# Rotary half-swap of the third layer: from a permuting matmul on TensorE to a 32-partition shuffle on VectorE, with the step positions written anew

## The chip, the cores and the metric

One core of a Trainium2 chip runs the whole program. The metric is device time in microseconds (us) of one launch; lower is better. Engines are named as in the profile: PE (TensorE matmuls) and PEld (its weight loads), DVE (VectorE), ACT (ScalarE), POOL (GpSimd), SP (the engine that issues all DMAs here).

## The reference

Four conditioned layers follow each other on `x` of 8 sequences x 256 tokens x 512 features, all in float32. The third layer (`L == 2` in the kernel) is the one whose rotary step changes:

```
h = layernorm(x) * (1 + scale) + shift          # layer 2, B=2, T=512 in the reference's shapes
q = (h @ Wq.T)      -> 16 heads x 32
k = ((h @ Wkd.T) @ Wku.T) -> 4 kv heads x 32 ;  v = ((h @ Wkd.T) @ Wvu.T)
q = q * cos + rotate_half(q) * sin              # rotate_half: [-x[16:], x[:16]] in each head of 32
k = k * cos + rotate_half(k) * sin
y = softmax(q k^T / sqrt(32) + block/window mask) v ;  x = x + y @ Wo.T
```

Layer 0 is attention with heads of 64 and rotary (`rotate_half` over 32 and 32 features) and a gated SiLU MLP, layer 1 is cosine attention and a GELU MLP, layer 3 is eight small expert MLPs of 64 features, a normalisation and a projection.

## The kernel before

Features lie on the partitions and tokens on the free axis: `X` is 128 partitions x 4 feature blocks x 2048 tokens. The work is cut into 12 attention **items** (`ORDER`: layer, block of 512 tokens) of 16 **units** each; a unit is one softmax of one token half of one head group. Layer 2's items are the 8th and the 10th to 12th: `(2,0)`, `(2,1)`, `(2,2)`, `(2,3)`. Around the units lie the MLPs of layers 0 and 1 and, for layer 2's blocks, the expert layer (`first`, `second`), its normalisation (`z`) and the last projection (`last`).

There is one list of **steps**. `Plan.make` gives each step a position in units (the table `PLACE`, plus the unit number), sorts by it, and each engine then walks the same list and emits its own part of each step. So the position of a step sets where its instructions stand in each in-order queue, and which piece of an engine's work stands in front of which. The names of steps: `scores`, `softmax`, `normalise`, `turn` (transposes of the probabilities on PE, copied to `PT`), `values` make up a unit; `ro1` projects q or k into a PSUM bank (`B`) which ACT copies to a buffer in SBUF (`FB`, seven of them); `ro2` is the rotary step; `qs` and `ks` split q and k into a rounded high part and a remainder (`Q`, `KB`); `nsum` to `nfin` are the pieces of a normalisation (`nsub` writes `Y`, `nfin` writes `HA`, `HM` or `ZH`/`ZL`). Within one unit the DVE part of `ro2` stands behind the four masked score maxima of a `softmax` (`CUSTOM_DVE_ANT_0`, printed as `ISA` in the order rows) and ahead of the next `normalise`, whose reciprocal POOL needs to scale the probabilities (`SS`) that PE then transposes.

The rotary step of layer 2 before the change, in the order of its queues:

```
PE   waits a_raw:        matmul(bank, rotm, f)        # rotm: a 128x128 permutation m <-> m ^ 16, plain f32
DVE  waits p_rot:        g = bank * sin
POOL waits p_rot:        f = f * cos                  # beside DVE
DVE  waits d_sin, g_cos: f = f + g
```

It runs 20 times: four q tiles and one k tile for each of four items, each on 128x512. In layer 0 the first two k and five q tiles (7) use the same form with a permutation of 32, and 13 others get their swap by DMA (`swap`, `s_swap`), so that there both products read two SBUF operands. `rotm` is loaded twice, at the start and, in step `tables`, again with layer 2's permutation.

Of the kernel before, what the change touches and what calls it, by code (L numbers as in the profile page):

```python
# [11 lines left out]
ALU = mybir.AluOpType  # L12
# [18 lines left out]
PLACE = {  # L31
# [6 lines left out]
    "trig": [3.589, 20.401, 35.517],  # L38
    "out": [17.616, 33.486, 49.609, 65.605, 81.749, 97.151, 113.474, 129.833, 145.534, 161.755, 177.973, 191.6,
        194.705],  # L40
    "first": [137.43, 169.635, 179.31, 193.854, 198.087],
    "z norm": [141.577, 174.923, 183.064, 198.2, 201.446],
    "z final": [144.398, 176.596, 185.493, 204.08, 205.384],
    "last": [145.545, 178.406, 187.993, 205.459, 209.491],
    "q0 first": [-0.458, 0.616],
    "k0 first": [-0.054, 2.293, 1.626, 3.239],
    "q0": [-0.46, 1.879, 2.452],
    "k0": [0.356, 0.84, 1.722, 2.736, 4.534],
    "v0": [1.914],
    "q1": [-1.273, 0.351, 1.427],  # L50
    "k1": [0.902, 1.089, 2.211, 2.301, 3.616],
    "v1": [3.958, 4.1],
    "q2": [0.073, 1.078],
    "k2": [-0.167, 0.282, 4.809, 2.078, 2.91],
    "v2": [1.691],
    "out 2": [-0.233, -0.229, 0.066, 0.655],
    "experts": [0.513, 0.533, 1.635, 1.133, 0.603],
    "experts of one": [0.1, 0.5, 0.9, 0.875, 0.856],
# [4 lines left out]
    "last step": [0.67, 0.474],  # L63
    "a stats": [0.101, 0.101, 1.31, 1.42, 1.42, 1.791, 1.598, 2.652],
    "m stats": [-0.005, -0.005, 1.086, 0.92, 0.904, 1.25, 1.163, 1.935],
    "a parts": [1.109, 0.01, 0.128, 0.03],
    "a parts 0": [0, -0.073, 0.02, 0.449],
    "m parts": [0, 0.01, 1.323, 0.145],
    "m parts 0": [0, 0.01, 0.02, 0.03],
    "down": [0.802],  # L70
    "start": [-12.43, 6, -2.831, -0.049],
    "ada": [7.843, 21.989, 25.511, 29.324, 31.58, 34.532, 37.145, 40.064, 43.72, 46.196, 49.144],
}
# [32 lines left out]
PIECE = _piece_numbers()  # L106
LATENT = ("latent", 2, 0)


# [68 lines left out]
class Engine:  # L178
# [44 lines left out]
    def reciprocal(self, *a, **k):  # L223
        return self.real.reciprocal(*a, **k) if self.real is not None else self  # L224

    def dma_start(self, *a, **k):
# [3 lines left out]
def halves(ap):  # L230
    return ap.rearrange("p (b s) -> p b s", b=2)
# [82 lines left out]
class Plan:  # L314
# [63 lines left out]
    def projected(self, what, L, n, t):  # L378
        k = (what, L, n, t)
        if what == "k" and L == 2:  # L380
            self.banked("kd", n)
            yield
        f = self.f.take()
        if L == 1:
            g = self.f.take()
            self.banked("un1", k, f, g)
            yield
            self.banked("un2", k, g)
            yield
            self.banked("un3", k, f, g)  # L390
            self.f.give(g)
        else:
            if what == "k" and L == 0:
                self.raw_values[n] = self.f.take()
                self.banked("kv", k, f, self.raw_values[n])
            else:
                self.banked("ro1", k, f)
            yield
            g = self.f.take()
            if swapped_by_dma(L, n, t):  # L400
                self.add("swap", k, f, g)
                yield
                self.add("ro2", k, f, g, None)
            else:
                self.banked("ro2", k, f, g)
            self.f.give(g)
        if what == "q":
            self.add("qs", k, f)
            self.f.give(f)
            yield  # L410
        else:
            yield
            self.add("ks", k, f, 0)
            yield
            self.add("ks", k, f, 1)
            self.f.give(f)
            yield
# [319 lines left out]
def program(nc, xT, pos, condT, biasd, cols, consts, tab2, wpack, adaw, out):  # L737
    ctx = ExitStack()
    with ctx:
# [3 lines left out]
        def tally(name, step=1):  # L743
            return Tally(ctx.enter_context(nc.semaphore(name)), step)
# [25 lines left out]
        rotm = sb("rotm", [128, 128])  # L770
# [14 lines left out]
        fr = Pool([FB[:, i, :] for i in range(FBUFS)])  # L785
# [3 lines left out]
        def col(name, i=0):  # L789
# [29 lines left out]
        d_nmul, d_nlo = tally("d_nmul"), tally("d_nlo")  # L819
        d_trig, d_sin, d_qk, d_qhi, d_khi = (tally(x) for x in ("d_trig", "d_sin", "d_qk", "d_qhi", "d_khi"))  # L820
        d_klo, d_qmax, d_ck = tally("d_klo"), tally("d_qmax"), tally("d_ck")
        d_max, d_neg, d_rec, d_pt, d_cx = (tally(x) for x in ("d_max", "d_neg", "d_rec", "d_pt", "d_cx"))
# [10 lines left out]
            a_y, d_ada, d_sm, d_gb, d_sum, d_sub, d_sq, d_var, d_nmul, d_nlo, d_trig,  # L833
            d_sin, d_qk, d_qhi, d_khi, d_klo, d_qmax, d_ck, d_max, d_neg, d_rec, d_pt, d_cx, d_xo, d_gate, d_glo,
            d_xd, d_tg, d_xl, g_const, g_whi, g_wlo, g_rstd, g_cos, g_qlo, g_qr, g_norm, g_xb]
# [113 lines left out]
        def tensor(e):  # L949
# [18 lines left out]
            for step in weights.steps:  # L968
# [65 lines left out]
                elif kind == "ro2":  # L1034
                    k, f, g, u = a
                    if u is not None:
                        e.wait_ge(*s_rot.of(k[1]))
                        e.wait_ge(*a_raw.of(*k))
                        e.wait_ge(*dp.over(u))
                        e.matmul(dp.buf(u)[:, :], rotm[:, :], fr.buf(f),  # L1040
                                 start=True, stop=True).then_inc(*p_rot.up(*k))
# [167 lines left out]
        def vector(e):  # L1209
            e.wait_ge(*s_cv.of())  # L1210
            e.wait_ge(*g_const.of(1))
            for step in weights.steps:
# [125 lines left out]
                elif kind == "ro2":  # L1338
# [5 lines left out]
                    e.wait_ge(*(a_sin.of(n) if L == 0 else s_tab.of()))  # L1344
                    if u is None:
                        e.wait_ge(*s_swap.of(*k))
# [354 lines left out]
        def gpsimd(e):  # L1701
            for step in weights.steps:
# [32 lines left out]
                elif kind == "ro2":  # L1735
# [4 lines left out]
                           TR[:, 0, 0:256].unsqueeze(1).broadcast_to([128, 2, 256]))  # L1740
                    e.wait_ge(*(p_rot if u is not None else s_swap).of(*k))
                    e.wait_ge(*(a_cos.of(n) if L == 0 else s_tab.of()))
# [26 lines left out]
        def sync(e):  # L1769
            for step in weights.steps:  # L1770
# [38 lines left out]
                elif kind == "tables":  # L1809
                    e.wait_ge(*d_qk.of("q", 0, 3, 3))  # L1810
                    e.dma_start(rotm[:, :], consts[2]).then_inc(*s_rot.up(2))
                    e.dma_start(TR[:, 0, :], tab2[0]).then_inc(*s_tab.up(0))
# [169 lines left out]
```

## Time and profile before

| what | value |
|---|---|
| runs of the kernel before | 2055.98, 2043.96, 2051.99 us; median 2051.99 |
| span of the profiled execution | 2053.7 us (the profile gives no other time for it) |
| PE busy, PEld busy | 1912.4 us (93%), 1512.5 us (74%) |
| DVE, ACT, POOL busy | 1110.8 (54%), 1027.7 (50%), 795.9 us (39%) |
| the chain that ended last, by engine | PE 76%, DVE 10%, POOL 4%, ACT 4%, issue 3%, DMA 1% |

The span is the time from the first to the last instruction of one execution. "Busy" is the share in which an engine had an instruction running. The chain is followed back from the last instruction, at each step to what released it; its shares say where a microsecond saved or added counts at once.

### The profile page before, as it was taken

How to read it: one execution, taken by the hardware profiler on the slowest of the kernel's cores; microseconds unless marked ns; L12 is line 12 of the kernel's file. 1: busy time of each engine (PE TensorE's matmuls, PEld its weight loads, DVE VectorE, ACT ScalarE, POOL GpSimd, SP SyncE). 2: the span in 40 equal slices, each digit the busy share in tenths (PEclk: the TensorE clock that was granted, in tenths of full speed). 3: DMA queues.
4: the chain of work that ended last, by engine and by line, in shares of the span. 5: the costliest groups of instructions: out<-in, count | busy, mean ns of one | idle time of the engine just before them, and what ended most of it. 6: DMA issues, size and time to landing. Idle time of an engine off the chain costs nothing.

```text
span 2053.7 us, 35242 instructions
## 1 busy us (share of the span) xinstructions
PE 1912.4 (93%) x12880; PEld 1512.5 (74%) x12880; DVE 1110.8 (54%) x3184; ACT 1027.7 (50%) x2474; POOL 795.9 (39%) x1094
## 2 busy tenths in 40 slices
PE   5889999999999999999899989989999989988987
PEld 3567777788888878887778777768876768855565
DVE  5655535644553365345664676574554675366363
ACT  3542423433343344443565465555567565468665
POOL 4556662111124243234667554326332432243230
PEclk9899999999999999999999999989999999989989
DMA  7336677555444534444345433433433335322311
GB/s 249 110 129 209 229 249 264 181 196 190 172 160 177 181 134 171 156 158 153 135 174 187 158 118 139 171 114 107 165 113 134 127 110 195 130 81 69 124 63 52
DMA packets 98795, 314.84 MB, mean 153 GB/s; under 512 B 11584, under 2 KB 13376, under 8 KB 97088
## 3 DMA queue, kind: packets, MB, share of 16 engines
q1 hardware_dynamic: 98624, 312.58, 43.7%
q8 instruction: 104, 1.70, 0.3%
q14 instruction: 67, 0.55, 0.1%
HBM read 242.55 MB, written 66.58 MB: 151 GB/s over the span
## 4 chain that ended last, share of the span: by engine, by line
PE 76%; DVE 10%; POOL 4%; ACT 4%; issue 3%; DMA 1%; SPq 0%; POOLq 0%; DVEq 0%; ACTq 0%
PE B L194 69%; PE B L197 7%; DVE FB L215 2%; POOL R L212 1%; DVE SS L218 1%; DVE T L212 1%; POOL SS L209 1%; ACT SS L200 1%; DVE FB L212 1%; POOL FB L212 1%; DMA ST<-in_wpack 1%; DVE PT L206 1%; ACT FB L200 1%; DVE HA L215 1%; POOL W L212 1%
## 5 line engine op out<-in xcount | busy, mean ns | idle before, releaser
L209 POOL TENSOR_SCALAR SS<-SS,NM 128x256 f32<-128x256 f32 (+1 forms) x640 | 290.2, 471 | 747.3 <-DVE NM L224 747.1
L194 PE MATMUL B<-HM,W 128*128 128x512 f32 x2304 | 540.1, 395 | 9.2 <-DVE HM L215 5.7
L194 PEld LDWEIGHTS B<-HM,W 128*128 128x128 f32 x2304 | 436.5, 190 | 105.6 <-issue 5.0
L194 PE MATMUL B<-G,W 128*128 128x512 f32 x1536 | 391.6, 405 | 8.1 <-POOL W L212 4.3
L194 PEld LDWEIGHTS B<-G,W 128*128 128x128 f32 x1536 | 286.1, 191 | 76.1 <-issue 10.7
L200 ACT ACTIVATE SS<-SS,NM 128x256 f32<-128x256 f32 (+1 forms) x512 | 240.5, 471 | 121.2 <-DVE NM L218 120.8
L194 PE MATMUL B<-HA,W 128*128 128x512 f32 x864 | 229.6, 418 | 6.1 <-DVE HA L212 4.4
L197 PE MATMUL B<-ident,SS 128*128 128x128 f32 x1152 | 180.6, 294 | 41.1 <-POOL SS L209 33.6
L194 PEld LDWEIGHTS B<-HA,W 128*128 128x128 f32 x864 | 170.6, 202 | 45.9 <-issue 5.4
L212 DVE TENSOR_TENSOR G<-FB,G 128x512 fp32r<-128x512 f32 x128 | 99.5, 780 | 165.3 <-ACT G L200 165.2
L197 PEld LDWEIGHTS B<-ident,SS 128*128 128x128 f32 x1152 | 129.9, 147 | 77.6 <-issue 41.1
L212 POOL TENSOR_TENSOR R<-R,few 128x16 f32<-128x16 f32 (+2 forms) x57 | 119.3, 2095 | 141.5 <-DVE R L209 141.4
L200 ACT ACTIVATE PT<-B 128x512 f32<-128x512 f32 x160 | 95.0, 593 | 149.6 <-PE B L197 147.4
L212 POOL TENSOR_TENSOR W<-ST,W 128x512 fp32r<-128x512 f32 x119 | 159.8, 1343 | 9.9
L200 ACT ACTIVATE G<-FB 128x512 fp32r<-128x512 f32 x128 | 80.9, 632 | 162.3 <-DVE FB L212 160.3
L209 POOL TENSOR_SCALAR W<-ST 128x512 fp32r<-128x512 f32 x119 | 80.3, 675 | 201.4 <-PE B L194 125.2
L212 DVE TENSOR_TENSOR FB<-FB,B 128x512 f32<-128x512 f32 x64 | 44.0, 687 | 191.5 <-PE B L194 175.8
L200 ACT ACTIVATE FB<-B 128x512 f32<-128x512 f32 (+2 forms) x148 | 85.6, 592 | 105.3 <-PE B L194 104.8
L194 PE MATMUL B<-CX,W 128*128 128x512 f32 (+1 forms) x624 | 136.3, 376 | 0.3 <-issue 0.3
L212 DVE TENSOR_TENSOR X<-X,B 128x512 f32<-128x512 f32 (+1 forms) x100 | 66.4, 665 | 128.8 <-PE B L194 128.7
L200 ACT ACT_TABLE_LOAD x99 | 127.0, 1283 | 4.8 <-PE B L194 2.4
L194 PEld LDWEIGHTS B<-CX,W 128*128 128x128 f32 x624 | 111.3, 190 | 22.8 <-issue 1.9
(109 smaller groups left out, 2654.0 us busy)
## 6 DMA issues: line engine op xcount, KB each, us to landing
W<-kept SPq DMA_DIRECT2D x357, 512.0 KB, 4.2
kept<-W SPq DMA_DIRECT2D x119, 512.0 KB, 4.6
ST<-in_wpack SPq DMA_DIRECT2D x139, 256.0 KB, 2.9
Y<-in_adaw SPq DMA_DIRECT2D x12, 1024.0 KB, 6.8
FB<-FB SPq DMA_DIRECT2D x52, 64.0 KB, 2.6
X<-in_xT SPq DMA_DIRECT2D x1, 3072.0 KB, 13.0
out_xT<-X SPq DMA_DIRECT2D x12, 256.0 KB, 2.1
FB<-in_pos SPq DMA_DIRECT2D x4, 256.0 KB, 6.0
```

Of the source, the lines that this page charges most:

```text
L194: return self.real.matmul(*a, **k) if self.real is not None else self
L197: return self.real.transpose(*a, **k) if self.real is not None else self
L200: return self.real.activation(*a, **k) if self.real is not None else self
L206: return self.real.tensor_copy(*a, **k) if self.real is not None else self
L209: return self.real.tensor_scalar(*a, **k) if self.real is not None else self
L212: return self.real.tensor_tensor(*a, **k) if self.real is not None else self
L215: return self.real.scalar_tensor_tensor(*a, **k) if self.real is not None else self
L218: return self.real.tensor_tensor_reduce(*a, **k) if self.real is not None else self
```

## The change

In layer 2 the PE matmul with `rotm` is gone. DVE swaps the halves itself with `stream_shuffle`, which permutes within each group of 32 partitions, from the buffer `f` into `g`, and then multiplies `g` by sin in place. POOL's product with cos now waits for the shuffle (it overwrites `f`, which the shuffle reads). The second load of `rotm` is gone. Layer 0 is as it was.

```diff
+SWAP_16 = [i ^ 16 for i in range(32)]
@@ Plan.projected
             if swapped_by_dma(L, n, t):
                 self.add("swap", k, f, g)
                 yield
                 self.add("ro2", k, f, g, None)
+            elif L == 2:
+                self.add("ro2", k, f, g, None)
             else:
                 self.banked("ro2", k, f, g)
@@ vector, step ro2
-                    if u is None:
+                    if L == 2:
+                        e.wait_ge(*a_raw.of(*k))
+                        e.wait_ge(*fr.over(gu))
+                        e.stream_shuffle(g, f, SWAP_16).then_inc(*d_swap.up(*k))
+                        e.wait_ge(*d_swap.of(*k))
+                        e.tensor_tensor(halves(g), halves(g), sin, ALU.mult).then_inc(*d_sin.up(*k))
+                    elif u is None:
@@ gpsimd, step ro2
-                    e.wait_ge(*(p_rot if u is not None else s_swap).of(*k))
+                    e.wait_ge(*(d_swap if L == 2 else p_rot if u is not None else s_swap).of(*k))
@@ sync, step tables
-                    e.dma_start(rotm[:, :], consts[2]).then_inc(*s_rot.up(2))
@@ PLACE (a few of the rows; nearly all changed by some hundredths to one unit)
-    "a norm": [3.377, 19.79, 36.916, ...
+    "a norm": [1.615, 20.526, 36.655, ...
-    "q0 first": [-0.458, 0.616],
+    "q0 first": [-0.361, 0.592],
-    "k1": [0.902, 1.089, 2.211, 2.301, 3.616],
+    "k1": [0.968, 1.082, 2.418, 2.301, 3.651],
-    "k2": [-0.167, 0.282, 4.809, 2.078, 2.91],
+    "k2": [-0.336, 1.352, 2.401, 1.944, 2.516],
-    "z stats": [-0.298, -0.298, 0.784, 0.657, 0.657, 1.406, 1.406, 2.27],
+    "z stats": [-0.319, -0.279, 0.835, 0.826, 0.567, 0.948, 1.536, 2.362],
-    "start": [-12.43, 6, -2.831, -0.049],
+    "start": [-12.532, 5.863, -1.544, 1.755],
```

The list of steps keeps its length; some 270 of the 2592 steps stand elsewhere, most of them by a few steps. Three places in DVE's queue are shown, all on one engine, since it is the one on which the new work lands.

**The start, first item.** DVE's queue from the first score maxima of unit 0 (`TENSOR_REDUCE NM<-B`) on. The first q tile is done; `FB<-B,TR` and what follows is the rotary step of the second q tile, `RECIPROCAL` is `normalise` of unit 0. Before:

```order
L221 TENSOR_REDUCE NM<-B 128x1 [waits p_sc]
L221 TENSOR_REDUCE NM<-B 128x1
L209 TENSOR_SCALAR NM<-NM 128x2 [waits d_max]
L212 TENSOR_TENSOR FB<-B,TR 128x512 [waits a_cos,p_rot]
L212 TENSOR_TENSOR FB<-FB 128x512 [waits g_cos,d_sin]
L206 CAST Q<-FB 128x512 [waits d_qk]
L224 RECIPROCAL NM<-NM 128x2 [waits a_exp]
```

and of the change:

```order
L222 TENSOR_REDUCE NM<-B 128x1 [waits p_sc]
L222 TENSOR_REDUCE NM<-B 128x1
L210 TENSOR_SCALAR NM<-NM 128x2 [waits d_max]
L225 RECIPROCAL NM<-NM 128x2 [waits a_exp]
L222 TENSOR_REDUCE NM<-B 128x1 x2
L210 TENSOR_SCALAR NM<-NM 128x2 [waits d_max]
L225 RECIPROCAL NM<-NM 128x2 [waits a_exp]
L222 TENSOR_REDUCE NM<-B 128x1 [waits p_sc]
L222 TENSOR_REDUCE NM<-B 128x1
L210 TENSOR_SCALAR NM<-NM 128x2 [waits d_max]
L213 TENSOR_TENSOR FB<-B,TR 128x512 [waits a_cos,p_rot]
```

The rotary step of the second q tile has moved from ahead of the first reciprocal to behind the second one.

**The k tile of the last item, (2,3).** DVE's queue at the last two of four score maxima of an even unit, then the rotary step of k and its split into `KB`. Before:

```order
L218 ISA SS,NM<-B,TR 128x128
L218 ISA NM 128x1
L212 TENSOR_TENSOR FB<-B,TR 128x512 [waits d_nlo,p_rot]
L212 TENSOR_TENSOR FB<-FB 128x512 [waits g_cos,d_sin]
L209 TENSOR_SCALAR KB<-FB 128x256 [waits d_qk]
L215 SCALAR_TENSOR_TENSOR KB<-FB,KB 128x256 [waits d_khi]
L209 TENSOR_SCALAR KB<-FB 128x256
L215 SCALAR_TENSOR_TENSOR KB<-FB,KB 128x256 [waits d_khi]
L224 RECIPROCAL NM<-NM 128x2 [waits a_exp] x2
```

and of the change, from the first q tile of the same item on:

```order
L228 STREAM_SHUFFLE FB<-FB 128x512 [waits a_raw]
L213 TENSOR_TENSOR FB<-FB,TR 128x512 [waits d_swap]
L213 TENSOR_TENSOR FB<-FB 128x512 [waits g_cos,d_sin]
L207 CAST Q<-FB 128x512 [waits d_qk]
L228 STREAM_SHUFFLE FB<-FB 128x512 [waits d_nlo,a_raw]
L213 TENSOR_TENSOR FB<-FB,TR 128x512 [waits d_swap]
L213 TENSOR_TENSOR FB<-FB 128x512 [waits g_cos,d_sin]
L225 RECIPROCAL NM<-NM 128x2 [waits a_exp] x2
L219 ISA SS,NM<-B,TR 128x128 [waits p_sc,g_norm]
L219 ISA NM 128x1
```

Each rotary step has one DVE instruction more, and k's stands one unit earlier, right behind q's; only its split into `KB` is left behind the score maxima.

**The second q tile of item (2,3).** DVE's queue from the rotary step on; `Y<-Y,B` are the four subtractions of the normalisation `z` of block 1. Before:

```order
L212 TENSOR_TENSOR FB<-B,TR 128x512 [waits d_nlo,p_rot]
L212 TENSOR_TENSOR FB<-FB 128x512 [waits g_cos,d_sin]
L206 CAST Q<-FB 128x512 [waits d_qk]
L212 TENSOR_TENSOR Y<-Y,B 128x512 [waits p_tot]
L212 TENSOR_TENSOR Y<-Y,B 128x512 x3
L224 RECIPROCAL NM<-NM 128x2 [waits a_exp] x2
```

and of the change:

```order
L228 STREAM_SHUFFLE FB<-FB 128x512 [waits d_nlo,a_raw]
L213 TENSOR_TENSOR FB<-FB,TR 128x512 [waits d_swap]
L213 TENSOR_TENSOR FB<-FB 128x512 [waits g_cos,d_sin]
L207 CAST Q<-FB 128x512 [waits d_qk]
L225 RECIPROCAL NM<-NM 128x2 [waits a_exp] x2
L219 ISA SS,NM<-B,TR 128x128 [waits p_sc,g_norm]
L219 ISA NM 128x1
```

The four subtractions have moved from ahead of the reciprocals to behind the next score maxima. At the same point of the next q tile but one, with block 2's subtractions, nothing has moved.

## Rows read from the trace of the kernel before

**Rows 1.** The page: span, and busy time by engine.

```profile
span 2053.7 us, 35242 instructions
PE 1912.4 (93%) x12880; PEld 1512.5 (74%) x12880; DVE 1110.8 (54%) x3184; ACT 1027.7 (50%) x2474; POOL 795.9 (39%) x1094
```

**Rows 2.** Windows: stretch, its length, busy us by engine, clock, DMA share, GB/s.

```profile
1240.00:1790.00 550.00, 527.35 (x3730) 415.71 (x3729) 315.89 (x1033) 318.11 (x786) 194.01 (x309) 0.97 0.39 138
1790.00:2054.00 264.00, 221.71 (x1669) 153.13 (x1667) 134.36 (x465) 172.43 (x443) 70.39 (x133) 0.90 0.23 77
```

**Rows 3.** Timeline of PE around two rotary matmuls: start, length, instruction.

```profile
1552.74 1.02 PE L194 MATMUL B<-FB,rotm 128*128 128x512 f32 x2
1553.69 1.13 PE L194 MATMUL B<-X,ST 64*128 64x512 f32 x4
...
1912.19 0.39 PE L194 MATMUL B<-ZH,W 128*128 128x512 f32 x1
1912.42 1.02 PE L194 MATMUL B<-FB,rotm 128*128 128x512 f32 x2
1912.87 0.80 PE L194 MATMUL B<-ZH,W 128*128 128x512 f32 x1
1913.51 0.40 PE L194 MATMUL B<-ZL,W 128*128 128x512 f32 x1
```

**Rows 4.** The chain that ended last, at rotary steps: start, length, engine.

```profile
1349.59 1.27 POOL FB L212
...
1801.60 0.61 DVE FB L212
...
1909.82 5.24 PE B L194 x21
...
1952.97 0.61 DVE FB L212
```

**Rows 5.** Timeline of DVE: two rotary steps of layer 2.

```profile
1852.28 0.69 DVE L212 TENSOR_TENSOR FB<-B,TR 128x512 f32<-128x512 f32 x1
1852.99 0.69 DVE L212 TENSOR_TENSOR FB<-FB 128x512 f32<-128x512 f32 x1
...
1913.47 0.69 DVE L212 TENSOR_TENSOR FB<-B,TR 128x512 f32<-128x512 f32 x1
1914.92 0.69 DVE L212 TENSOR_TENSOR FB<-FB 128x512 f32<-128x512 f32 x1 [0.76 <-POOL FB L212]
```

**Rows 6.** Timeline of DVE and POOL: two rotary steps of layer 0 after a DMA swap.

```profile
117.51 0.68 DVE L212 TENSOR_TENSOR FB<-FB,TR 128x512 f32<-128x512 f32 x1
117.55 1.80 POOL L212 TENSOR_TENSOR FB<-FB,TR 128x512 f32<-128x512 f32 x1
...
240.22 1.29 POOL L212 TENSOR_TENSOR FB<-FB,TR 128x512 f32<-128x512 f32 x1 [2.15 <-DMA FB<-FB]
240.24 1.82 DVE L212 TENSOR_TENSOR FB<-FB,TR 128x512 f32<-128x512 f32 x1 [0.63 <-DMA FB<-FB]
```

**Rows 7.** Groups by line and form: busy us, mean ns of one, idle before.

```profile
L206 DVE COPY PT<-B 128x512 f32<-128x512 f32 x128 | 87.7, 685 | 39.6 <-PE B L197 39.5
L206 DVE CAST Q<-FB 128x512 fp32r<-128x512 f32 x48 | 20.6, 428 | 1.6
```

**Rows 8.** Timeline of PE: the first transposes of probabilities.

```profile
46.16 1.11 PE L197 MATMUL B<-ident,SS 128*128 128x128 f32 x4 [3.78 <-POOL SS L209]
```

**Rows 9.** The chain at the second rotary step of item (2,3).

```profile
1877.90 2.47 DVE Y L212 x4
```

**Rows 10.** The chain ahead of the first up-projection of layer 1.

```profile
980.32 0.97 DVE KB L209
...
981.95 0.87 DVE FB L215 x2
```

**Rows 11.** Timeline of DVE: the k tile of item (2,3).

```profile
1861.81 0.29 DVE L218 CUSTOM_DVE_ANT_0 SS<-B,TR 128x128 f32<-128x128 f32 x1 [7.53 <-PE B L194]
...
1863.14 0.69 DVE L212 TENSOR_TENSOR FB<-B,TR 128x512 f32<-128x512 f32 x1 [0.39 <-PE B L194]
```

More of the change, by code:

```diff
@@ L31 @@
 PLACE = {
[6 rows of a table removed]
[L38 to L44, printed above, removed]
-    "q0 first": [-0.458, 0.616],
-    "k0 first": [-0.054, 2.293, 1.626, 3.239],
@@ L47 @@
[L47 to L50, printed above, removed]
-    "k1": [0.902, 1.089, 2.211, 2.301, 3.616],
-    "v1": [3.958, 4.1],
-    "q2": [0.073, 1.078],
-    "k2": [-0.167, 0.282, 4.809, 2.078, 2.91],
[L55 to L58, printed above, removed]
[4 rows of a table removed]
-    "last step": [0.67, 0.474],
-    "a stats": [0.101, 0.101, 1.31, 1.42, 1.42, 1.791, 1.598, 2.652],
@@ L65 @@
[L65 to L69, printed above, removed]
[6 rows of a table added]
+    "trig": [3.757, 20.79, 35.346],
+        "out": [17.562, 33.986, 49.665, 65.869, 81.465, 97.161, 114.6, 129.42, 145.624, 161.915, 178.22, 191.644,
+        194.786],
+    "first": [137.423, 169.635, 179.31, 193.787, 198.265],
+    "z norm": [140.957, 175.185, 183.101, 198.014, 201.221],
@@ new lines @@
+    "z final": [144.289, 176.77, 185.552, 203.718, 205.5],
+    "last": [145.658, 178.299, 187.993, 206.303, 209.503],
+    "q0 first": [-0.361, 0.592],
+    "k0 first": [-0.233, 2.603, 1.16, 3.296],
+    "q0": [-0.503, 1.822, 2.318],
+    "k0": [0.161, 0.313, 1.159, 2.7, 4.778],
+    "v0": [1.932],
+    "q1": [-1.242, 0.3, 1.457],
+    "k1": [0.968, 1.082, 2.418, 2.301, 3.651],
+    "v1": [3.967, 4.146],
+    "q2": [0.145, 1.054],
+    "k2": [-0.336, 1.352, 2.401, 1.944, 2.516],
+    "v2": [1.589],
@@ new lines @@
+    "out 2": [-0.25, -0.2, 0.3, 0.6],
+    "experts": [0.515, 0.535, 1.5, 1.135, 0.605],
+    "experts of one": [0.075, 0.228, 0.851, 0.829, 0.818],
[4 rows of a table added]
+    "last step": [0.67, 0.355],
+    "a stats": [0.082, 0.144, 1.119, 1.387, 1.337, 1.78, 1.579, 2.691],
+    "m stats": [-0.14, 0.078, 1.086, 0.825, 0.904, 1.25, 1.16, 1.992],
+    "a parts": [0.863, 2.514, 1.443, -0.016],
+    "a parts 0": [1.686, -0.064, -0.015, 0.53],
+    "m parts": [0.008, -0.048, 1.986, 0.187],
+    "m parts 0": [-0.021, 0.957, 0.919, 0.038],
@@ L70 @@
     "down": [0.802],
-    "start": [-12.43, 6, -2.831, -0.049],
-    "ada": [7.843, 21.989, 25.511, 29.324, 31.58, 34.532, 37.145, 40.064, 43.72, 46.196, 49.144],
+    "start": [-12.532, 5.863, -1.544, 1.755],
+    "ada": [8.231, 22.321, 26.715, 29.81, 31.968, 34.92, 37.498, 40.455, 44.123, 46.8, 49.75],
 }
@@ L224, in reciprocal, with stream_shuffle @@
         return self.real.reciprocal(*a, **k) if self.real is not None else self
+    def stream_shuffle(self, *a, **k):
+        return self.real.stream_shuffle(*a, **k) if self.real is not None else self
     def dma_start(self, *a, **k):
@@ L820, in program @@
         d_trig, d_sin, d_qk, d_qhi, d_khi = (tally(x) for x in ("d_trig", "d_sin", "d_qk", "d_qhi", "d_khi"))
+        d_swap = tally("d_swap")
         d_klo, d_qmax, d_ck = tally("d_klo"), tally("d_qmax"), tally("d_ck")
@@ L833, in program @@
             a_y, d_ada, d_sm, d_gb, d_sum, d_sub, d_sq, d_var, d_nmul, d_nlo, d_trig,
-            d_sin, d_qk, d_qhi, d_khi, d_klo, d_qmax, d_ck, d_max, d_neg, d_rec, d_pt, d_cx, d_xo, d_gate, d_glo,
+            d_swap, d_sin, d_qk, d_qhi, d_khi, d_klo, d_qmax, d_ck, d_max, d_neg, d_rec, d_pt, d_cx, d_xo, d_gate, d_glo,
             d_xd, d_tg, d_xl, g_const, g_whi, g_wlo, g_rstd, g_cos, g_qlo, g_qr, g_norm, g_xb]
@@ L1036, in tensor @@
                     if u is not None:
-                        e.wait_ge(*s_rot.of(k[1]))
+                        e.wait_ge(*s_rot.of(0))
                         e.wait_ge(*a_raw.of(*k))
@@ L1950 @@
         np.full((128, 1), math.pi / 2), np.tile(np.repeat([-1.0, 1.0], 32), 2)[:, None]], axis=1)
-    consts = np.zeros((3, 128, 128), f)
+    consts = np.zeros((2, 128, 128), f)
     consts[0] = np.eye(128)
     for m in range(128):
-        consts[1, m ^ 32, m] = consts[2, m ^ 16, m] = 1.0
+        consts[1, m ^ 32, m] = 1.0
     i = np.arange(256)
```

18 rows, old and new, of the table PLACE are left out of this document.

## The prediction

> **What bounds the kernel now.** I read the page first, then the windows by stage, then the chain of waits at each of the 20 places that the change touches, then the timeline there. The page says that PE has a matmul running in 93% of the 2053.7 us and no other engine in more than 54% [rows 1]. So a removed matmul is worth its time wherever PE has no wait close by, and DVE has room on average. The windows correct this for the end: from 1240 to 1790 us PE is busy 527 of 550, but after 1790 us, where no MLP work is left to fill in, PE is busy 222 of 264 us [rows 2], and the waits there are for one unit's softmax to go around DVE, ACT, POOL and PE. The profiled execution's only own time is its span of 2053.7 us; the median of the runs shown is 1.7 us less, so I make the sum against the span and take 1.7 off. The three runs spread over 12 us, so about 0.5% (10 us) is what a measurement of this kernel can tell from no change.
>
> **What the change takes from PE.** One swap is two matmul instructions on 128x512, 20 swaps in all. The busy time of 1.02 us overlaps with its neighbours, so I take the delay of the next work. Around 1912 us the instruction before the swap gave way after 0.23 us, the swap itself after 0.45, and the first product behind it after 0.64 in place of 0.23: 0.45 + 0.64 - 0.23 = 0.86 us. Where a plain f32 product follows, as at 1552.74, it starts 0.95 us after the swap [rows 3]. I looked up the chain at all 20 places: at 14 the swap lies inside a stretch of the chain on PE (the last of them is the stretch at 1909.82), at six (1347, 1596, 1799, 1819, 1873 and 1949 us) it doesn't [rows 4]. Of the 14, ten are of the first kind and four of the second: 10 x 0.86 + 4 x 0.95 = **-12.4 us**. For the other six I take nothing, since PE waits for DVE or POOL there anyway; all twenty at 0.95 would be -19, the far end. The second load of `rotm` held up nothing; nothing for that.
>
> **What it adds on DVE.** Before, DVE is held for one rotary step from the start of its product to the end of its sum. This comes in two sizes: 1852.28 to 1853.68 is 1.41 us where POOL had its product done before (14 of the 20), and 1913.47 to 1915.61 is 2.14 us where the sum waits 0.76 for POOL (6 of 20) [rows 5]. The change makes all 20 alike, because POOL's product can't start before DVE's shuffle is done. The trace has no shuffle. The nearest rows are the 128x512 copy from PSUM with 685 ns and the 128x512 cast within SBUF with 428 ns [rows 7]; I take 0.69, because nothing shows that a permutation runs at the cast's rate, and keep 0.43 as the low end.
>
> Behind the shuffle, both products read two SBUF operands and are released by the same semaphore. That is what layer 0 does after its DMA swaps, and its rows show that the two then don't run side by side: at 117.51 DVE starts first, and POOL's product, elsewhere 1.29 us, takes 1.80; at 240.22 POOL starts 0.02 earlier, and DVE's product, elsewhere 0.68, takes 1.82 [rows 6]. In the first case POOL ends at 119.35, and with 0.10 to the sum and its 0.69 the pair and the sum take 2.63 us; in the second DVE ends at 242.06, and they take 2.54. Before the change, DVE's product in layer 2 read PSUM and ran beside POOL's without loss. So a rotary step will hold DVE for 0.69 + 0.05 + 2.6 = **3.3 us**, which is 1.9 more in the 14 cases and 1.2 more in the six: 14 x 1.9 + 6 x 1.2 = 34 us of DVE time. Were the products side by side, it would be 0.69 + 0.05 + 1.29 + 0.10 + 0.69 = 2.8.
>
> The Trainium skill ("SBUF — State Buffer", the part on the two physically separate sides) has the rule behind this: VectorE and GpSimd share one pair of SBUF ports, an instruction of VectorE with two SBUF inputs takes it as an exclusive lock against a GpSimd instruction that reads SBUF, and the later one blocks until the earlier has ended. By that rule the sum below has 8.8 us for DVE; with 2.8 us per step, which one would take without it, it would have 6.3. The trace agrees with the rule in layer 0, with 1.80 and 1.82 us.
>
> **Where DVE's extra time counts.** The reciprocal for POOL and the split for the scores stand behind each step, so it counts where the chain runs through the rotary step. That is so at 1349, 1801, 1821, 1863, 1876 and 1952 us [rows 4]. The first was of the longer kind, +1.2; four of the rest were of the shorter, 4 x 1.9 = 7.6; together **+8.8 us**. The one at 1863 is k's, which is moved (below). At the other 14 I price it at nothing: the chain there is on PE's products, which run on while DVE is held. If that cover is gone everywhere, it is the full 34.
>
> **What the moved steps bring.** The shift of all places goes both ways, and I price only those that stand at a PE wait.
> - Start: PE waits 3.78 us for the first scaled probabilities [rows 8]. The reciprocal in front of them stood behind a rotary step of 2.1 us and a cast of 0.43 [rows 5, 7]; it no longer does: -2.6, between 0 and -2.6, because a projection of 12 matmuls has moved into the same wait.
> - Up-projection of layer 1 at 986 us: the chain runs through a split of k for 1.6 us, from 980.32 to 981.95 [rows 10]. By the new `k1` and `m final` it stands behind the first two parts of the normalisation: -1.6, or 0 if the second part is then late by as much.
> - The four subtractions at 1877.90, 2.5 us on the chain [rows 9], stand behind reciprocals and maxima now: -2.5.
> - k of the last item: its wait of 0.39 and its step of 2.1 us lay on the chain; one unit earlier it falls into an idle time of DVE of 7.5 us, of which it needs 3.3 [rows 5, 11]: -2.5.
>
> Sum of these: **-9.2**, from 0 to -9.2. SP's queue has the large load of `X` one place earlier and one load less; no wait of PE is on either.
>
> **The sum.** -12.4 + 8.8 - 9.2 = -12.8 us: 2053.7 - 12.8 = 2040.9 as a span, less 1.7 is **2039 us**, 0.6% faster.
>
> **The rivals.**
> 1. *The forecast*: PE's time is saved at some two thirds of the places, DVE gives part of it back at five, the moves repair the worst. 2039; its own range 2031 to 2045. Chance 0.45.
> 2. *The moved steps bring nothing.* Half of the list's shifts have no row that speaks for them, and a wait that goes from one place can come back one unit later. Without the 9.2: 2053.7 - 12.4 + 8.8 - 1.7 = 2048, within 0.5%. For it: two of my four prices are upper bounds. Chance 0.27.
> 3. *DVE's cost is hidden almost everywhere and the moves help more than I can price.* -19 + 0 - 9.2 gives 2024; halfway between this and the forecast 2031. For it: DVE has 46% idle, and a whole table of places was set to suit the new lengths. Chance 0.18.
> 4. *DVE becomes the bound of layer 2's units* (the other side). Place: each rotary step of (2,0) to (2,3), ahead of the reciprocal that POOL waits for and PE's transposes behind it. It decides once PE's queue behind those transposes is shorter than the 1.9 us added. PE's idle time after 1790 us is already 42 us in 264 [rows 2]. If 34 us count in full against 12.4 and the moves bring 0: 2053.7 + 21.6 - 1.7 = 2074; if two thirds of it do, +10, 2062. Against it: between 1240 and 1790 us PE is idle for 23 of 550 us only [rows 2], and at 11 of the 13 rotary steps there the chain is on PE. Chance 0.10.
>
> That the change doesn't do what it says I exclude: DVE's queue has 20 shuffles and PE's 20 rotary matmuls fewer. The range takes the first three rivals and half of the way to the fourth: 2026 to 2055. From the cases, faster by over 0.5% (below 2041.7) has 0.18 + two thirds of 0.45 + a little of rival 2 = 0.53, within 0.5% 0.37, slower 0.10.
>
> **What would show it.** Right: 14 `rotm` matmul instructions are left of 54; PE's busy time falls by about 20 us; a shuffle takes about 0.69 us; DVE's or POOL's product behind it takes 1.8 in place of 0.69 or 1.3; from shuffle to the end of the sum 3.3 us in all 20. PE's wait at 46 us is shorter by 2 to 3 us, and that at 986 by up to 1.6. Wrong: the shuffle is 1 us or more (each 0.3 us is 1.5 on the path, six in all); PE's idle time in 1240 to 1790 us grows from 23 us by more than 5, which is rival 4; or the stretch 120 to 1240 us, where nothing of the swap lies, is longer by more than 3 us, which would mean that the moved steps hurt.

## The result, and the profile after

The changed kernel takes 2061.64 us (median of 4 runs, 2059.84 to 2063.22) where the kernel before takes 2047.97 (median of 4, 2042.92 to 2055.98): ratio 1.0064, 95% interval [1.0037, 1.0091]. It is slower by 0.6%, some 13 us. The forecast was 2039 us with a range that ended at 2055. A span is about 2 us shorter than its launch (2059.8 against 2061.57 here), so the profiled execution of before, with a span of 2053.7 us, is the longest of its four launches, 8 us above their median. So the two spans differ by only 6 us; for sizes I use medians and ratios.

The page of the changed kernel: span, busy time, and the chain that ended last by engine.

```profile
span 2059.8 us, 35190 instructions
PE 1891.5 (92%) x12840; PEld 1499.2 (73%) x12840; DVE 1130.3 (55%) x3224; ACT 1027.1 (50%) x2474; POOL 802.5 (39%) x1094
...
PE 72%; DVE 11%; POOL 5%; ACT 4%; issue 4%; DMA 2%; SPq 0%; DVEq 0%; POOLq 0%; ACTq 0%
```

PE is busy 21 us less than in [rows 1] and yet the span is longer. The windows say where its idle time grew (columns as in [rows 2]).

```profile
1240.00:1790.00 550.00, 516.57 (x3664) 407.76 (x3664) 321.71 (x1047) 318.25 (x793) 200.60 (x307) 0.97 0.40 138
1790.00:2059.80 269.80, 215.00 (x1642) 148.71 (x1640) 139.96 (x478) 170.01 (x433) 71.91 (x130) 0.88 0.24 75
```

PE's idle time is 33.4 us in the first stretch (before 22.7) and 54.8 in the second (before 42.3). That is 23 us more, and more than the 21 us by which PE's busy time fell. The cast to `Q` behind the first rotary step of item (2,0) starts at 1243.50 (before 1246.05), so the changed kernel enters layer 2 with a lead of 2.6 us; the one behind the last step of (2,3) starts at 1960.49 (before 1954.33). All of the loss comes in between.

The new instructions, by source line (duration in ns: shortest, median, longest), and who waited for them:

```profile
L228 DVE LOAD_MASK_SELECT FB<-FB x20: 12/14/15, 1240.1 to 1957.1; - x20
L228 DVE STREAM_SHUFFLE FB<-FB x20: 721/732/752, 1240.1 to 1957.1; 128x512 f32<-128x512 f32 x20
...
  POOL FB L213: 55.2, 18
```

Timeline of DVE and POOL at the rotary step that [rows 5] shows first:

```profile
1852.40 0.01 DVE L228 LOAD_MASK_SELECT FB<-FB  x1
1852.40 0.74 DVE L228 STREAM_SHUFFLE FB<-FB 128x512 f32<-128x512 f32 x1
...
1853.17 0.69 DVE L213 TENSOR_TENSOR FB<-FB,TR 128x512 f32<-128x512 f32 x1
...
1853.22 1.77 POOL L213 TENSOR_TENSOR FB<-FB,TR 128x512 f32<-128x512 f32 x1 [12.14 <-DVE FB L228]
...
1855.10 0.69 DVE L213 TENSOR_TENSOR FB<-FB 128x512 f32<-128x512 f32 x1 [1.23 <-POOL FB L213]
```

From the start of the shuffle to the end of the sum DVE is held 3.39 us (1852.40 to 1855.79), before 1.41. Over the 20 steps it is 3.37 to 3.94, in sum 69.5 us (before 32.5): 37 us more. I call this sum the **held time** below.

What a longer hold does is seen at 1801 us of [rows 4]. The chain of the changed kernel, from the last score maximum ahead of the rotary step to the transposes behind it:

```profile
1798.13 0.28 DVE SS L219
1798.42 0.73 DVE FB L228
1799.15 0.07 issue
1799.22 1.78 POOL FB L213
...
1801.10 0.70 DVE FB L213
...
1801.83 0.44 DVE Q L207
...
1802.33 1.27 POOL Q L213
1803.60 3.12 POOL SS L210 x4
...
1806.77 1.55 PE B L198 x6
```

Product and sum took 1.33 us of the chain before (0.61, 0.02 and 0.70); the same stretch is now 3.38 us, from 1798.42 to 1801.80, and it also pushes POOL's scaling of the probabilities (`SS`). PE's timeline shows the wait at two of these places:

```profile
1805.01 0.69 PE L198 MATMUL B<-ident,SS 128*128 128x128 f32 x2 [3.61 <-POOL SS L210]
...
1826.79 0.69 PE L198 MATMUL B<-ident,SS 128*128 128x128 f32 x2 [4.52 <-POOL SS L210]
```

Before, PE waited 0.85 and 1.96 us there. In the list of waits of the whole execution the same pairs have grown: for PE's transposes from 33.6 us in 21 waits, for the rotary sum from 24.2, for ACT's exponentials behind the masked maxima from 120.8:

```profile
ACT SS L201 <- DVE NM L219: 148.8, 96, 6.2
...
DVE FB L213 <- POOL FB L213: 44.2, 30, 8.8
...
PE B L198 <- POOL SS L210: 39.7, 24, 6.5
```

### The profile page after: what moved, and what is told of

Same layout as the page of the kernel before. It is cut to its first block, busy times and chain, and to the rows that moved or that the text cites. A ratio compares the mean times of both kernels' runs of the same rounds, so it can differ in the third digit from the quotient of the medians.

```text
span 2059.8 us, 35190 instructions
## 1 busy us (share of the span) xinstructions
PE 1891.5 (92%) x12840; PEld 1499.2 (73%) x12840; DVE 1130.3 (55%) x3224; ACT 1027.1 (50%) x2474; POOL 802.5 (39%) x1094
## 4 chain that ended last, share of the span: by engine, by line
PE 72%; DVE 11%; POOL 5%; ACT 4%; issue 4%; DMA 2%; SPq 0%; DVEq 0%; POOLq 0%; ACTq 0%
PE B L195 66%; PE B L198 6%; DVE SS L219 2%; POOL FB L213 2%; DVE FB L216 2%; DMA ST<-in_wpack 1%; POOL SS L210 1%; POOL R L213 1%; DVE T L213 1%; ACT SS L201 1%; DVE PT L207 1%; ACT FB L201 1%; DVE FB L213 1%; POOL W L213 1%; DVE X L216 1%
## 5 line engine op out<-in xcount | busy, mean ns | idle before, releaser
L195 PE MATMUL B<-HA,W 128*128 128x512 f32 x864 | 223.9, 409 | 9.8 <-DVE HA L213 4.5
L195 PEld LDWEIGHTS B<-HA,W 128*128 128x128 f32 x864 | 165.9, 197 | 48.7 <-issue 4.2
```

What stands on the lines that cost most here:

```text
L195: return self.real.matmul(*a, **k) if self.real is not None else self
```

## The experiments

My theory after the result: the time for which DVE is held decides, at all 20 steps and not only at the five that I priced; removed PE time and moved steps bring less than I took them for. The rival: the new places of the steps cost what the shuffle gains. Ratios are to the kernel before, with 95% intervals; 0.001 is 2.05 us, and "held" in a result is the held time of the 20 steps in that run's trace.

### The two halves of the change apart

`e1_places` is the kernel before with the new table `PLACE`; `e2_shuffle` is the changed kernel with the old table.

> The kernel before with the new table of places and nothing else: the matmul swap stays. Theory P (the new places lose time by themselves): ratio to before at 1.005 or more, most of the measured 1.0064. Theory D (the places are about neutral or a small gain, and the rotary step on VectorE costs more than TensorE saves): 0.995 to 1.001, and the PE waits that the prediction priced are shorter (46 us by 2 to 3 us, 986 us by 1 to 2, the one after 1877 us by 2).

> The changed kernel with the table of places of before: the shuffle alone. Theory D: slower than before, 1.003 to 1.010, with PE's busy time down by 20 us and PE's idle time up by more than that, most of it after 1240 us; a rotary step holds DVE for 3.3 us. Theory P: 0.992 to 0.998, since 12 us of TensorE time are gone from the path and DVE has room.

Measured: places alone **1.0001** [0.9988, 1.0014], shuffle alone **1.0086** [1.0064, 1.0108]. The rival is out: the places cost nothing that can be told (the interval is 2.7 us either way), and the whole loss is the shuffle's, with 69.2 us held. With the new places it is 1.0064; the intervals overlap, so whether they repair some of it isn't told.

### What the removed matmul is worth, and what an added one costs

`e3_narrow` keeps the rotary matmul of layer 2, on 64 of its 512 columns (the swap of the other columns is left out); `e12_double` does it twice.

```diff
@@ tensor, step ro2 (e3_narrow)
-                        e.matmul(dp.buf(u)[:, :], rotm[:, :], fr.buf(f),
+                        z = slice(0, 64) if k[1] == 2 else slice(0, 512)
+                        e.matmul(dp.buf(u)[:, z], rotm[:, :], fr.buf(f)[:, z],
@@ tensor, step ro2 (e12_double)
+                        if k[1] == 2:
+                            e.matmul(dp.buf(u)[:, :], rotm[:, :], fr.buf(f), start=True, stop=True)
```

> The kernel before, with layer 2's 20 rotary matmuls on 64 of their 512 columns (the other columns of the bank are then not the swapped halves, so this part of the computation is left out); DVE and POOL do what they did. It takes about seven eighths of the 18 us off TensorE and adds nothing anywhere. If the prediction's 12.4 us on the path is right: 0.994 to 0.996 (8 to 12 us faster). If TensorE's time is mostly not on the path (the removed matmuls are given back as waits at once): 0.998 to 1.001.

> The kernel before with each of layer 2's 20 rotary matmuls done twice on PE (the same result), so 18 us more on TensorE and nothing else. If 14 of the 20 are on the path, as the prediction read from the chain: +12 us, 1.005 to 1.007. If the narrow matmul told right that only a quarter to a third of such time counts: +4 to +6 us, 1.002 to 1.003.

Measured: 7/8 of the matmul away **0.9981** [0.9966, 0.9996], -3.9 us for 15 to 17 us of PE (7/8 of 20 x 0.86 to 0.95); done twice **1.0071** [1.0052, 1.0091], +14.6 us for 17 to 19. By this run my -12.4 was about three times too large. Per microsecond of PE the two directions differ (0.25 and 0.8), by more than their intervals allow.

### The hold of DVE, shortened with the shuffle kept

POOL's product with cos goes to a third buffer. It needs no longer wait for the shuffle, only for `a_raw`, and has ended when DVE comes. `e4_third` has the old places, `e5_third_places` the new, and `e8_before_third` is the kernel before with the third buffer.

```diff
@@ e5_third_places against the changed kernel; some lines left out
-                self.add("ro2", k, f, g, None)
+                h = self.f.take()
+                self.add("ro2", k, f, g, h)
+                self.f.give(h)
@@ vector, step ro2
-                    e.tensor_tensor(f, f, g, ALU.add).then_inc(*d_qk.up(*k))
+                    e.tensor_tensor(f, fr.buf(u) if L == 2 else f, g, ALU.add).then_inc(*d_qk.up(*k))
@@ gpsimd, step ro2
-                    e.wait_ge(*(d_swap if L == 2 else p_rot if u is not None else s_swap).of(*k))
+                    e.wait_ge(*(a_raw if L == 2 else p_rot if u is not None else s_swap).of(*k))
-                    e.tensor_tensor(halves(f), halves(f), cos, ALU.mult).then_inc(*g_cos.up(*k))
+                    if L == 2:
+                        e.wait_ge(*fr.over(u))
+                    e.tensor_tensor(halves(fr.buf(u)) if L == 2 else halves(f), halves(f), cos, ALU.mult).then_inc(*g_cos.up(*k))
```

> As the shuffle alone with before's places, but POOL writes its product with cos into a third buffer of FB, so it waits for the copy of the projection and not for the shuffle, and mostly runs before DVE gets there. A rotary step then holds DVE for about 0.73 + 0.69 + 0.69 = 2.2 us in place of 3.3. Theory D with the port lock and the late product of POOL as the larger part: at least 8 us faster than the shuffle alone and no slower than before (0.994 to 1.000). If the shuffle's own time or the places are to blame: within 3 us of the shuffle alone.

> The changed kernel, places and all, with POOL's product in a third buffer. If the places are neutral here as they were with the matmul swap: like the third buffer with before's places, 0.997 to 1.001, so 10 to 17 us faster than the changed kernel. If the new places suit a long rotary step and no other: 1.002 to 1.006.

> The kernel before, matmul swap and places kept, with POOL's product in a third buffer and waiting for the copy of the projection only. The six rotary steps in which DVE waited 0.76 us for POOL lose that wait: at most 4.5 us less holding. Theory D1: 0.998 to 1.000. It also says how much of the third buffer's gain is POOL's and how much is that the shuffle needs it.

Timeline of DVE in `e4_third`, at the same step as above:

```profile
1845.60 0.73 DVE L228 STREAM_SHUFFLE FB<-FB 128x512 f32<-128x512 f32 x1
...
1846.36 0.69 DVE L213 TENSOR_TENSOR FB<-FB,TR 128x512 f32<-128x512 f32 x1
...
1847.09 0.69 DVE L213 TENSOR_TENSOR FB<-FB 128x512 f32<-128x512 f32 x1
```

The hold is 2.18 us here (1845.60 to 1847.78), 47.0 in all, and the loss is gone: **0.9997** [0.9979, 1.0015]. With the new places it is 0.9993 [0.9980, 1.0005] (held 48.9), and the third buffer in the kernel before gives 0.9998 [0.9987, 1.0010]. So 22 us less of held time went with 18 us less of time: 0.8 each. None of the three can be told from the kernel before. Two things change at once here: DVE is held less, and POOL's product is done early and no longer stands late in POOL's own queue, ahead of its scaling of the probabilities. These runs don't separate the two.

### The hold lengthened with the matmul kept

In `e6_copy_late` DVE copies the matmul's bank to `g` ahead of its product, and POOL waits for the copy, as it does for the shuffle; in `e7_copy` POOL waits for the matmul as before.

```diff
@@ vector (e6_copy_late and e7_copy)
+                        if L == 2:
+                            e.tensor_copy(g, dp.buf(u)[:, :]).then_inc(*d_swap.up(*k))
+                            e.wait_ge(*d_swap.of(*k))
@@ gpsimd (e6_copy_late only)
-                    e.wait_ge(*(p_rot if u is not None else s_swap).of(*k))
+                    e.wait_ge(*(d_swap if L == 2 else p_rot if u is not None else s_swap).of(*k))
```

> The kernel before with the matmul swap kept, and in layer 2 one DVE copy of the bank to SBUF ahead of the product with sin, for which POOL's product waits as it does for the shuffle. The product with sin still reads the bank in PSUM, so two long products with two SBUF operands never meet: the late product of POOL without the port lock. A rotary step should hold DVE for about 2.8 us. Theory D1 (DVE's holding time is what costs, whatever it is made of; 17.6 us at +34 to +37 us of holding, plus what TensorE gave back): with +24 us of holding about 13 us slower than before, 1.005 to 1.008. Theory D2 (the lock has an effect beyond its time): under 1.004.

> As the run with the copy, but POOL's product waits for the matmul as before. Only 20 x 0.7 us of DVE time are added; DVE is held for 2.1 us in the cases that were short, and for 2.1 to 2.8 in the others. Theory D1: about 6 to 8 us slower than before, 1.002 to 1.005. If DVE's 46% of idle time hides it, as the prediction priced the places off the chain: under 1.002.

Timeline of DVE and POOL in `e6_copy_late`:

```profile
1848.94 0.69 DVE L206 COPY FB<-B 128x512 f32<-128x512 f32 x1
1849.66 0.69 DVE L212 TENSOR_TENSOR FB<-B,TR 128x512 f32<-128x512 f32 x1
1849.71 1.27 POOL L212 TENSOR_TENSOR FB<-FB,TR 128x512 f32<-128x512 f32 x1 [13.44 <-DVE FB L206]
1851.09 0.69 DVE L212 TENSOR_TENSOR FB<-FB 128x512 f32<-128x512 f32 x1 [0.73 <-POOL FB L212]
```

Held 57.4 us in all: **1.0053** [1.0033, 1.0073]; `e7_copy`, held 43.1: **1.0032** [1.0020, 1.0044]. With no shuffle and nothing taken from PE, 25 and 11 us more of held time cost 11 and 7 us. `e7_copy` leaves POOL's instructions and their waits as they were, so it is the run that shows DVE's hold alone to cost. POOL's late start adds 4.3 us in `e6_copy_late`, which the intervals don't tell from nothing.

### Where in layer 2 it costs

`e10_first_two` shuffles only in (2,0) and (2,1), `e11_last_two` only in (2,2) and (2,3); the old places.

```diff
@@ against the shuffle everywhere; SHUFFLED is (0, 1) or (2, 3)
-            elif L == 2:
+            elif L == 2 and n in SHUFFLED:
```

> Shuffle in items (2,0) and (2,1) only, before's places, matmul swap in the other two. The shuffle everywhere cost 17.6 us. The prediction priced four of the six critical rotary steps in the last two items, so by it at most a quarter of the cost, about 2 us net or a gain, falls here: 0.998 to 1.002. If the cost falls evenly on all rotary steps, on or off the chain: 1.003 to 1.006.

> The other half: shuffle in items (2,2) and (2,3) only. By the prediction's places most of the cost is here: 1.004 to 1.008. If even: 1.003 to 1.006. The two halves should add up to 1.0086 unless one hides the other.

Measured: **1.0056** [1.0040, 1.0071] and **1.0036** [1.0016, 1.0056], in sum 0.0092 against 0.0086 for both. The first half is the one in which PE has little idle time (before, it is busy 437 of 460 us from 1240 to 1700, 95%) and where I priced one step of ten. It costs 11.5 us for 18 us more of held time, the other 7.4 for 18; the intervals overlap, so which half costs more isn't told. In `e10_first_two` PE is idle 34.4 us from 1240 to 1790, before 22.7.

### The sum on POOL

`e9_pool_sum` is `e5_third_places` with the sum of the products on POOL and the split of q 0.6 units later.

```diff
@@ gpsimd, step ro2; other lines left out
+                    if L == 2:
+                        e.wait_ge(*d_sin.of(*k))
+                        e.wait_ge(*g_cos.of(*k))
+                        e.tensor_tensor(f, fr.buf(u), fr.buf(gu), ALU.add).then_inc(*g_add.up(*k))
```

> A try for a version that beats both: the shuffle with the third buffer and the new places, and in layer 2 the sum of the two products moved from DVE to POOL, q's split 0.6 unit later so that DVE need not wait for it. DVE's rotary work falls to shuffle and one product, 1.4 us per step, as little as the kernel before had, and TensorE's swap is gone. If a microsecond of DVE time costs 0.45 as the runs so far say: 0.996 to 0.999. If POOL's sum (1.3 us, ahead of its scaling of probabilities) takes DVE's place in the wait: 1.000 to 1.004.

Measured: **0.9997** [0.9982, 1.0011], no gain over `e5_third_places`, with POOL busy 31 us more (823.7 against 792.7). DVE is rid of the sum, but the cast behind it on the same queue still waits, 1.38 us, for POOL's sum:

```profile
1847.34 0.69 DVE L213 TENSOR_TENSOR FB<-FB,TR 128x512 f32<-128x512 f32 x1
1849.41 0.43 DVE L207 CAST Q<-FB 128x512 fp32r<-128x512 f32 x1 [1.38 <-POOL FB L213]
```

### PE and DVE in one table

Both products and the sum of layer 2 on 64 of 512 columns (the rotation of the other 448 is left out), with the matmul in full (`e13`), on 64 columns (`e14`), twice (`e15`), and with the shuffle in full (`e16`, old places).

```diff
+                    z = slice(0, 32) if L == 2 else slice(0, 256)
@@ the sum; both products are cut to z in the same way
-                    e.tensor_tensor(f, f, g, ALU.add).then_inc(*d_qk.up(*k))
+                    e.tensor_tensor(halves(f)[:, :, z], halves(f)[:, :, z], halves(g)[:, :, z], ALU.add).then_inc(*d_qk.up(*k))
```

> The kernel before with layer 2's product with sin, product with cos and sum on 64 of 512 columns, on DVE and POOL; the rotary matmul is kept in full. Left out: the rotation of the other 448 columns. DVE is then held for some 0.3 us per rotary step where it was 1.63 on average, so 24 to 26 us less in all. If a microsecond of DVE held counts in both directions alike, at the 0.45 to 0.6 that the added ones cost, the time falls by 11 to 15 us: 0.993 to 0.995. If it only costs when it is added, because PE is the bound once DVE is early, it falls by 0 to 4 us: 0.998 to 1.000.

> As the kernel before with narrow vector work, and the rotary matmul on 64 columns too. Left out: swap and rotation of the other 448 columns. If PE's removed time brought only 4 us because DVE's queue was next in line, it brings its 12 now: some 24 us below the kernel before, 0.987 to 0.990. If it is lost to something else, such as other waits of PE or the granted clock, it lies 4 us below the kernel with narrow vector work alone.

> The kernel before with the rotary matmuls of layer 2 done twice and the vector work of the rotary step on 64 of 512 columns (the rotation of the other 448 is left out). If 18 us more of PE cost the same 12 to 15 us whatever DVE does, this lies 12 to 15 us above the kernel with narrow vector work alone. If the repeated matmul had cost because DVE and POOL started their products later, it lies 5 us above or less.

> The shuffle in full, with the places of before, and both products and the sum on 64 of 512 columns (the rotation of the other 448 is left out). DVE is held for about 1.1 us per step, 22 us in all, 10 less than before the change, and PE has 18 us less. If the loss of the shuffle is the time for which DVE is held, this is 4 to 9 us below the kernel before: 0.9955 to 0.998. If the shuffle costs by itself, or by PE's missing work and the idle time and clock that follow it, it is at 1.000 or above.

| rotary matmul | DVE full | held, us | DVE narrow | held, us |
|---|---|---|---|---|
| on 64 columns | 0.9981 [0.9966, 0.9996] | 31.8 | 0.9957 [0.9942, 0.9972] | 9.9 |
| once | 1 | 32.5 | 0.9996 [0.9982, 1.0010] | 10.9 |
| twice | 1.0071 [1.0052, 1.0091] | 37.5 | 1.0045 [1.0029, 1.0061] | 11.0 |
| none, shuffle | 1.0086 [1.0064, 1.0108] | 69.2 | 0.9992 [0.9977, 1.0006] | 30.9 |

Timeline of DVE and POOL in `e16_shuffle_vec`:

```profile
1846.87 0.72 DVE L228 STREAM_SHUFFLE FB<-FB 128x512 f32<-128x512 f32 x1
...
1847.63 0.22 DVE L213 TENSOR_TENSOR FB<-FB,TR 128x64 f32<-128x64 f32 x1
1847.68 0.36 POOL L213 TENSOR_TENSOR FB<-FB,TR 128x64 f32<-128x64 f32 x1 [8.35 <-DVE FB L228]
1848.14 0.23 DVE L213 TENSOR_TENSOR FB<-FB 128x64 f32<-128x64 f32 x1 [0.28 <-POOL FB L213]
```

Three things follow. With DVE's hold at 10 us, less PE time is worth 8.0 us and more costs 10.0, about 0.5 per us in both directions. That is 4 us more than `e3_narrow` gained, as if DVE had kept part of its gain back, but the difference is uncertain by 5 us, so this isn't shown. The hold taken away with PE's work kept brings nothing that can be told (0.9996, 0.8 us, uncertain by 3); that is 22 us of held time at next to no price, where I had expected 11 to 15 us if it counted alike. And the shuffle in full with a hold as short as before costs nothing (0.9992), so it isn't the shuffle itself that costs, nor that PE's swap is missing; the 4 to 9 us that I expected it to gain didn't come either.

In order of held time, with PE relieved of the swap: 9.9 us 0.9957, 30.9 and 31.8 us 0.9992 and 0.9981, 47.0 us 0.9997, 69.2 us 1.0086. With the swap on PE: 10.9 us 0.9996, 32.5 us 1, 43.1 us 1.0032, 57.4 us 1.0053. The price of a microsecond is not one number. By these values, and with POOL's product changing along with the hold in several of them, it is about 0.2 with PE relieved between 10 and 47 us held and 0.8 above; with the swap kept it is nothing below 32 us and 0.45 to 0.6 above.

## Why the prediction was wrong, by its own steps

**What bounds the kernel.** I read the chain of waits at 20 places and took "the chain is on PE" to mean that DVE has slack there. The chain shows which wait ended last, not by how much. `e10_first_two` shows that the slack in (2,0) and (2,1) was in sum far below what the steps added: 11.5 us of time for 18 us of hold, though PE had 10 of its 20 swaps fewer.

**PE, -12.4 us: mis-sized.** The counts were right (14 `rotm` matmul instructions are left, PE's busy time fell by 21 us), the price was not. `e3_narrow` gives -3.9 for 7/8 of it; with DVE's hold nearly gone it is 8.0 (`e14` against `e13`). A removed microsecond of PE is worth 0.25 to 0.5 us here, not the 0.7 that 14 of 20 places at full price came to. Part of it turns into idle time: between the cast to `Q` behind the first rotary step of (2,1) and that behind the last of (2,3) PE is idle for 34.1 us in `e3_narrow` and for 29.5 before.

**DVE per step, 3.3 us: right.** The shuffle took 732 ns (taken: 0.69), POOL's product 1.77 (1.80), the step 3.48 on average (3.3), so 37 us more in place of 34. The 2.8 us that I gave for products side by side is what `e6_copy_late` has (57.4 / 20 = 2.87), where DVE's product reads PSUM. At two steps POOL is still at the split of q (`Q<-FB,Q`) when DVE's product starts; then that product is long, and POOL's product with cos behind it is long too. Timeline of DVE and POOL at the k tile of (2,3):

```profile
1856.18 0.73 DVE L228 STREAM_SHUFFLE FB<-FB 128x512 f32<-128x512 f32 x1
1856.33 1.27 POOL L213 TENSOR_TENSOR Q<-FB,Q 128x512 fp32r<-128x512 f32 x1 [1.34 <-DVE Q L207]
...
1856.95 1.20 DVE L213 TENSOR_TENSOR FB<-FB,TR 128x512 f32<-128x512 f32 x1
1857.56 1.72 POOL L213 TENSOR_TENSOR FB<-FB,TR 128x512 f32<-128x512 f32 x1
1859.39 0.69 DVE L213 TENSOR_TENSOR FB<-FB 128x512 f32<-128x512 f32 x1 [1.24 <-POOL FB L213]
```

**Where DVE's time counts, +8.8 us: the step that failed.** The forecast said: "At the other 14 I price it at nothing: the chain there is on PE's products, which run on while DVE is held." They did not run on for long enough. `e2_shuffle` is +17.6 us as a whole, and with 4 to 8 us of PE's saving in it the longer step has cost 22 to 26, where 8.8 were forecast. That lies near the two thirds of rival 4, to which I gave a chance of 0.10. That its 2062 and the measured 2061.64 agree is luck: it stood on a base of 2052 and a loss of 10 us, with -12.4 for PE; the four launches give a base of 2048 and a loss of 13 to 14. The test that I had named for it also came true: PE's idle time in 1240 to 1790 us grew by 10.8 us, with 5 as the limit.

**The moved steps, -9.2 us: wrong in sum (`e1_places`: 0).** Two of the four waits went away and came back elsewhere. The first transposes of probabilities wait no more, but PE's wait ahead of the first scores has grown from 3.44 us (at 37.56) to 6.84, because the projection of 12 matmuls that now stands in front of the transposes had filled it; `e1_places` shows the same with 6.76. The three waits behind the transposes, 3.8 us together, take the place of two of before, 0.35 and 3.07. Over the first 120 us PE is idle for 39.2 us (before 37.8). Timeline of PE, changed kernel:

```profile
40.19 1.65 PE L195 MATMUL B<-KB,Q 64*128 64x256 f32 x12 [6.84 <-issue]
...
46.69 0.66 PE L198 MATMUL B<-ident,SS 128*128 128x128 f32 x4
...
48.94 0.65 PE L198 MATMUL B<-ident,SS 128*128 128x128 f32 x4 [0.73 <-POOL SS L210]
...
53.21 0.98 PE L195 MATMUL B<-KB,Q 64*128 64x256 f32 x12 [0.87 <-POOL Q L213]
...
57.01 1.87 PE L195 MATMUL B<-FB,rotm 128*128 128x512 f32 x2 [2.16 <-ACT FB L201]
```

The up-projection of layer 1 starts 9.2 us after the first piece of its normalisation on the chain (980.09 to 989.26), before 11.7 (979.61 to 991.30): the -1.6 was real, even -2.5, and makes up the lead at the start of layer 2. The third, the four subtractions, is still on the chain, behind the next score maxima:

```profile
1882.57 2.39 DVE Y L213 x4
```

They now hold up the normalisation's statistics in place of the probabilities. With the matmul kept (`e1_places`) PE's waits at this place are 5.3 us where they were 6.4. The fourth, k one unit earlier, puts two rotary steps in a row on DVE, 1852.40 to 1860.08, and the first scaled probabilities behind them come 4.8 us later (POOL's `SS` at 1860.25, before 1855.46); PE hardly waits for them there. That is my rival 2, which was right about the moves but not about DVE.

**The clock.** I had no term for it. The granted clock of 1790 us to the end is 0.88 after, 0.87 in `e2_shuffle`, 0.90 before [rows 2] and 0.90 in `e13_narrow_vec`. It fell around PE's waits: about the one of 4.52 us that ended at 1826.79 the changed kernel has most of 11 us at the lower level, 1.2 GHz, and is back at 2.4 GHz from 1836 on. Windows of the changed kernel, clock as a share of 2.4 GHz:

```profile
1814.00:1825.00 11.00, 6.87 (x101) 5.11 (x99) 8.03 (x37) 5.84 (x21) 6.44 (x11) 1.00 0.14 48
1825.00:1836.00 11.00, 7.35 (x23) 5.24 (x24) 9.35 (x34) 7.41 (x25) 4.05 (x9) 0.53 0.01 2
1836.00:1846.00 10.00, 8.56 (x59) 4.78 (x60) 1.99 (x13) 7.61 (x19) 3.23 (x8) 1.00 0.33 105
```

Before, the like stretch was 7 us long (1826 to 1833, clock 0.51), at the end of a wait of 1.96 us. Summed from 1240 us on in steps of 4 us, clock withheld (1 minus the granted share, times the length) is 39 to 44 us in the profiles of before, `e1`, `e8` and `e12`, 49 after and 56 in `e2_shuffle`. But `e4_third` has 51 and `e16_shuffle_vec` 49 without a loss, and `e6_copy_late` and `e7_copy` lose 11 and 7 us with 44 and 41. So a lower clock can carry a few microseconds of the shuffle's loss, and how many is open; the hold of DVE costs without it.

**What stays open.** The table's four differences for PE's time (-3.9, -8.0, +14.6, +10.0, each uncertain by 3 to 5 us) are not explained by one price per microsecond; `e12_double` has 5 us more of held time, which is part of its +14.6. How much of the shuffle's 22 to 26 us is DVE's hold and how much POOL's late and longer product isn't separated; only the hold is shown to cost alone (`e7_copy`). Why 22 us of held time bring 1 us when taken away with the swap on PE, and 5 us when it is not (if the two differ at all: their difference is uncertain by 5 us), I can only argue: two rings through a unit, PE's own queue and the way around DVE, ACT and POOL, of which only the longer counts. No version here that computes the same is faster than the kernel before; the best, `e5_third_places`, beats the changed kernel by about 0.7% and ties with before.

## What to carry to other kernels

Work moved from the busiest engine to one that is half idle isn't free: before you price it at nothing, ask how long the receiving engine's in-order queue is held, from the first new instruction to the last wait, and what stands behind it. A busy share of 96% on one engine and a chain that runs through it don't show the slack of the others; measure it, with a dummy copy in the queue (as in `e7_copy`, where 11 us of hold cost 7 us of time), before writing the real thing. When such a move loses, look first at which wait lengthens the hold: here one buffer more for POOL's product won back the 18 us.

## What the runs showed of the hardware

- A `stream_shuffle` of 128x512 f32 within SBUF takes 732 ns and its mask load 14 ns: close to the copy from PSUM of the same size with 685 [rows 7], not to the cast within SBUF with 428.
- VectorE's product with two SBUF operands and GpSimd's beside it: when VectorE starts first, VectorE's takes 0.69 us and GpSimd's 1.77. When GpSimd is still at another product with SBUF operands, VectorE's takes 1.20 and ends 0.55 us after that one (1857.60 to 1858.15). With one operand of VectorE's product in PSUM, released by the same kind of event in `e6_copy_late`, GpSimd's takes 1.27. The Trainium skill ("SBUF — State Buffer", the part on the two physically separate sides) says that two such instructions share a pair of ports of which the first to start has the whole, and that the other one waits until it has ended. The trace agrees but for a little: a full wait would make 0.64 + 1.27 = 1.91 us of GpSimd's 1.77 (an estimate from the rows at 1853.17 and the 1.27).
- From 1240 us on the granted clock of the changed kernel fell to the lower level during PE's waits or behind them, and the longest such stretch outlasted its wait: in the changed kernel the clock is 0.52 from 1962 to 1976 us around a wait of 5.52 that ended at 1964.47, though PE is busy 10.4 of these 14 us.
